# Copying and starting x's quarters one by one, and computing the last 128 tokens by tokens, in a conditioned residual block on one core

## The reference

```python
x = x + causal_depthwise_conv(x, cond[:, None, :])        # 32 taps, taps shared by all sequences
ada = (cond @ ada_w + ada_b)[:, None, :]
shift1, scale1, gate1, shift2, scale2, gate2 = split(ada, 6)
x1 = ln(x) * (1 + scale1) + shift1
q, k, v = split(x1 @ qkv_w + qkv_b)                       # 16 heads of 128
attn = softmax(q k^T / sqrt(128)) v                       # within a sequence of 32 tokens
x = x + gate1 * (attn @ out_w + out_b)
x2 = ln(x) * (1 + scale2) + shift2
h = gelu(x2 @ ffn_w1 + ffn_b1)                            # 1024 hidden channels
x = x + gate2 * (h @ ffn_w2 + ffn_b2)
```

## Time and profile before

| | us |
|---|---|
| median of 3 runs | 304.48 (304.09 to 304.70) |
| the profiled execution's own time | 304.34 |
| its span in the trace | 302.5 |
| PE busy | 295.8 |
| DVE busy | 183.0 |
| ACT busy | 171.4 |
| POOL busy | 121.8 |
| last product of TensorE starts | 298.06 |

### The profile page before, as it was taken

How to read it: one execution, slowest core, us unless ns; L and a number is a source line. 1 busy time by engine, 2 the same in 40 slices (tenths; PEclk the granted TensorE clock), 3 DMA queues, 4 the chain that set the end, 5 groups by cost and what they waited for, 6 DMA issues and landing times.

```text
span 302.5 us, 6172 instructions
## 1 busy us (share of the span) xinstructions
PE 295.8 (98%) x2598; PEld 250.0 (83%) x2598; DVE 183.0 (60%) x323; ACT 171.4 (57%) x310; POOL 121.8 (40%) x104
## 2 busy tenths in 40 slices
PE   7999999999999999999999999999999999999994
PEld 7896898878898888788888888888888888877884
DVE  3997697997867648472446664350721364859533
ACT  5953377534862765485267736644763695624910
POOL 5207839331811553172337134630916381321410
PEclk9999999999999999999999999999999999999998
DMA  7912422400250061007003400520090000000404
GB/s 227 367 41 71 119 91 70 142 0 2 62 217 0 4 210 71 0 2 277 3 2 111 168 0 2 177 103 0 4 339 8 2 0 3 0 1 2 69 0 69
DMA packets 22427, 23.00 MB, mean 76 GB/s; under 512 B 9240, under 2 KB 15488, under 8 KB 22400
## 3 DMA queue, kind: packets, MB, share of 16 engines
q1 hardware_dynamic: 20720, 22.39, 22.6%
q10 hardware_dynamic: 1680, 0.23, 0.4%
HBM read 21.57 MB, written 1.05 MB: 75 GB/s over the span
## 4 chain that ended last, share of the span: by engine, by line
PE 85%; DVE 11%; POOL 1%; issue 1%; ACT 0%; DVEq 0%; POOLq 0%
PE bank L1051 16%; PE bank L1052 16%; PE bank L1053 16%; PE bank L1139 8%; DVE xc L591 6%; PE bank L1059 5%; PE bank L1061 5%; PE bank L1060 5%; PE bank L1123 3%; PE bank L1267 3%; PE bank L1269 2%; PE bank L1268 2%; DVE pt L741 1%; DVE ol L746 1%; POOL wl L314 1%; PE bank L1010 1%
## 5 line engine op out<-in xcount | busy, mean ns | idle before, releaser
L314 POOL TENSOR_TENSOR wl<-raw,wh 128x512 fp32r<-128x512 f32 x70 | 96.0, 1396 | 119.2 <-ACT wh L387 100.8
L442 ACT ACTIVATE pool<-bank,bT 128x512 f32<-128x512 f32 x56 | 38.5, 688 | 50.4 <-PE bank L1053 50.4
L1051 PE MATMUL bank<-x1h,wl 128*128 128x512 f32 (+1 forms) x180 | 66.8, 371 | 0.0
L1052 PE MATMUL bank<-x1l,wh 128*128 128x512 f32 (+1 forms) x180 | 65.7, 365 | 0.0
L1053 PE MATMUL bank<-x1h,wh 128*128 128x512 f32 (+1 forms) x180 | 65.6, 365 | 0.0
L746 DVE SCALAR_TENSOR_TENSOR ol<-bank,bT,oh 128x512 fp32r<-128x512 f32 x32 | 23.9, 749 | 31.6 <-ACT oh L467 30.8
L591 DVE SCALAR_TENSOR_TENSOR xc<-x,condT,xc 128x496 f32<-128x496 f32 (+27 forms) x76 | 39.9, 593 | 0.1
L387 ACT ACTIVATE wh<-raw 128x512 fp32r<-128x512 f32 x70 | 39.8, 622 | 0.0
L1051 PEld LDWEIGHTS bank<-x1h,wl 128*128 128x128 f32 x180 | 34.0, 189 | 6.4 <-issue 1.0
L1053 PEld LDWEIGHTS bank<-x1h,wh 128*128 128x128 f32 x180 | 34.0, 189 | 5.5
L1052 PEld LDWEIGHTS bank<-x1l,wh 128*128 128x128 f32 x180 | 34.0, 189 | 5.0
(11 more groups left out here) (136 smaller groups left out, 426.0 us busy)
## 6 DMA issues: line engine op xcount, KB each, us to landing
raw<-in_L_cond_qkv_w_dram SPq DMA_DIRECT2D x24, 512.0 KB, 5.7
raw<-in_L_cond_out_w_dram SPq DMA_DIRECT2D x8, 512.0 KB, 3.6
raw<-in_L_cond_ffn_w_dram SPq DMA_DIRECT2D x3, 512.0 KB, 7.0
adaw<-in_L_cond_ada_w_dram SPq DMA_DIRECT2D x1, 1024.0 KB, 10.3
out_dram<-pool SPq DMA_DIRECT2D x12, 64.0 KB, 1.9
xtok<-in_x_dram SPq DMA_DIRECT2D x2, 256.0 KB, 3.1
adaw<-in_L_cond_ada_w_dram SPq DMA_DIRECT2D x1, 512.0 KB, 5.2
xtok<-in_x_dram SPq DMA_DIRECT2D x1, 512.0 KB, 6.0
```

Source lines behind the costliest of these rows:

```text
L314: g.tensor_tensor(wl[:, cols], raw[:, cols], wh[:, cols].bitcast(F32), ALU.subtract)\
L442: a.activation((q_sb if j < GH else k_sb)[:, j % GH, :], src, ACT.Identity, bias=bias(U, j // GH, j % GH)).then_inc(s_ev, 1)
L1051: pe.matmul(dst, wl[:, w_cols], a_hi, start=start, stop=False)
L1052: pe.matmul(dst, wh[:, w_cols], a_lo, start=False, stop=False)
```

## The change

Two changes are made at once. At the start, each of the four pieces of x (two quarters times two channel groups) gives its own signal when it is turned; the second quarter is turned into banks `PB[0]` and `PB[2]`. VectorE copies only the first piece, ScalarE the other three. VectorE then runs the first lag (lag 0) as four steps of 256 tokens, and TensorE its first lag (lag 13) as four products of 256 tokens, each behind its own piece. TensorE's three idle products go.

At the end, the last 128 tokens (the last four sequences) are taken out of pieces 2 and 3, which now cover 384 tokens each, and the old piece 4 goes. In its place `ffn2_last` multiplies the other way round: `hh` and `hl` of the 128 tokens are the stationary operand, the weights' 256 columns move, and the result has tokens as rows. What it has to be multiplied by and added to must then have tokens as rows too: `last_rest_by_blocks` on VectorE makes gate2 times bias plus residual for the 128 tokens, and transposes that and gate2 in blocks of 32 x 32, between hidden tiles 5 and 7; 16 transfers from SBUF to SBUF, all on SP, put the blocks in their places (`pexp`). The result is then one multiplication and one addition over 256 columns, and is stored by two transfers of 64 rows of 1 KB each, one on SP and one on ScalarE's queue. No transpose follows.

```diff
-        ALL, FRONT, BACK = slice(0, HT), slice(0, HT // 2), slice(HT // 2, HT)
-        FFN2_PIECES = [(0, 0, YB[0][:, ALL], ALL), (0, 1, YB[1][:, ALL], ALL), (1, 0, YB[0][:, ALL], ALL),
-                       (1, 1, YB[1][:, FRONT], FRONT), (1, 1, PB[0][:, FRONT], BACK)]
+        X_BANKS = [OB, (PB[0], PB[2])]
+        ALL, FRONT, BACK = slice(0, HT), slice(0, HT - P), slice(HT - P, HT)
+        FFN2_PIECES = [(0, 0, YB[0][:, ALL], ALL), (0, 1, YB[1][:, ALL], ALL), (1, 0, YB[0][:, FRONT], FRONT),
+                       (1, 1, YB[1][:, FRONT], FRONT)]
+        last_turned = pn[:, :].rearrange("p (q f) -> p q f", q=2 * CT)
+        last_rest, last_gate, last_rows = pe_[:, 0:C], pe_[:, C:2 * C], sd[:, 0:C]
...
 @block.sync
-            for n, ct in ((0, 0), (0, 1), (1, 0)):
-                sp.wait_ge(s_turn, CT * n + ct + 1)
+            for ct in range(CT):
+                sp.wait_ge(s_turn, ct + 1)
                 for i in range(P // T):
-                    store_blocks(sp, n, ct, i, ALL)
-            sp.wait_ge(s_turn, 5)
+                    store_blocks(sp, 0, ct, i, ALL)
+            sp.wait_ge(s_lturn, 2 * CT)
+            for b in range(QB):
+                for i in range(P // T):
+                    sp.dma_start(pe_[T * b:T * (b + 1), :].rearrange("t (q i c) -> t q i c", i=P // T, c=T)[:, :, i, :],
+                                 last_turned[T * i:T * (i + 1), :, T * b:T * (b + 1)]).then_inc(s_lrows, 16)
+            sp.wait_ge(s_turn, 3)
+            for i in range(P // T):
+                store_blocks(sp, 1, 0, i, FRONT)
+            sp.wait_ge(s_turn, 4)
             for i in range(2):
-                store_blocks(sp, 1, 1, i, BACK)
+                store_blocks(sp, 1, 1, i, FRONT)
+            sp.wait_ge(s_fin, 5)
+            store_last(sp, 0)
...
 @block.scalar
-            for n in range(2):
-                a.wait_ge(s_xt, n + 1)
-                a.activation(part(x0, 1, CHUNKS[n]), (OB, YB)[n][1][:, 0:256], ACT.Copy).then_inc(s_xe[1], 1)
+            for n, ct in ((0, 1), (1, 0), (1, 1)):
+                a.wait_ge(s_xt, CT * n + ct + 1)
+                a.activation(part(x0, ct, CHUNKS[n]), X_BANKS[n][ct][:, 0:256], ACT.Copy).then_inc(s_xe[1], 1)
...
 @block.vector
+            v.tensor_copy(part(x0, 0, CHUNKS[0]), X_BANKS[0][0][:, 0:256]).then_inc(s_xe[0], 1)
             for n in range(2):
-                v.wait_ge(s_xt, n + 1)
-                v.tensor_copy(part(x0, 0, CHUNKS[n]), (OB, YB)[n][0][:, 0:256]).then_inc(s_xe[0], 1)
-                if n == 0:
-                    first_lag(0)
+                for ct in range(CT):
+                    if (n, ct) == (0, 0):
+                        v.wait_ge(s_xe[0], 1)
+                    else:
+                        v.wait_ge(s_xe[1], CT * n + ct)
+                    xs = part(x0, ct, CHUNKS[n])
+                    v.scalar_tensor_tensor(out=part(xc, ct, CHUNKS[n]), in0=xs, scalar=condT[:, ct, T - 1:T], in1=xs,
+                                           op0=ALU.mult, op1=ALU.add).then_inc((s_cfirst, s_cdve)[n], 1)
...
+            def last_rest_by_blocks():
+                for ct in range(CT):
+                    v.scalar_tensor_tensor(out=rest, in0=ada(GATE2, ct, LAST_SPAN),
+                                           scalar=bT[:, B_F2 + ct:B_F2 + ct + 1],
+                                           in1=by_batch(part(xc, ct, LAST_SPAN)), op0=ALU.mult, op1=ALU.add)\
+                        .then_inc(s_lbias, 1)
+                    v.wait_ge(s_lbias, ct + 1)
+                    v.transpose(by_batch(last_turned[:, ct, :]), rest).then_inc(s_lturn, 1)
+                    v.transpose(by_batch(last_turned[:, CT + ct, :]), ada(GATE2, ct, LAST_SPAN)).then_inc(s_lturn, 1)
...
-            gated(4)
-            turn(4)
+            v.wait_ge(s_f2, 5)
+            v.wait_ge(s_lrows, 16 * QB * P // T)
+            v.tensor_tensor(last_rows, LAST_BANK, last_gate, ALU.mult).then_inc(s_gt, 1)
+            v.wait_ge(s_gt, 5)
+            v.tensor_tensor(last_rows, last_rows, last_rest, ALU.add).then_inc(s_fin, 1)
...
 @block.tensor
-                m.then_inc(s_xt, 1)
+                    m.then_inc(s_xt, 1)
-            idle_products(3)
...
+            def first_lag():
+                j = PE_LAGS[0][0]
+                for n in range(2):
+                    for ct in range(CT):
...
+                        t0 = CHUNKS[n][0]
+                        pe.matmul(by_batch(CONV_BANK[0][ct][:, t0:t0 + 256])[:, :, j:], diag[:, ct, :],
+                                  by_batch(part(x0, ct, CHUNKS[n]))[:, :, :T - j], start=(n == 0), stop=False)
...
-            conv(0, 0, 6)
+            first_lag()
+            conv(0, 1, 6)
...
+            def ffn2_last(k):
+                pe.matmul(LAST_BANK, hh[:, k, BACK], w_lo, start=(k == 0), stop=False)
+                pe.matmul(LAST_BANK, hl[:, k, BACK], w_hi, start=False, stop=False)
+                m = pe.matmul(LAST_BANK, hh[:, k, BACK], w_hi, start=False, stop=(k == MT - 1))
```

More of the change, by code:

```diff
@@ L227, in store_blocks, with store_last @@
                 .then_inc(s_out, 16)
+        def store_last(eng, i):
+            rows_i = slice(i * P // 2, (i + 1) * P // 2)
+            eng.dma_start(out[B_LAST:B].rearrange("b t c -> (b t) c")[rows_i], last_rows[rows_i]).then_inc(s_out, 16)
         block = ctx.enter_context(nc.Block())
@@ L550, in _ @@
             a.wait_ge(s_turn, 4)
-            for i in range(P // T):
+            for i in range(2, P // T):
                 store_blocks(a, 1, 1, i, FRONT)
-            a.wait_ge(s_turn, 5)
-            for i in range(2, P // T):
-                store_blocks(a, 1, 1, i, BACK)
+            a.wait_ge(s_fin, 5)
+            store_last(a, 1)
         @block.vector
@@ L561, in _ @@
                 .then_inc(s_cond, 1)
[L562 to L574 removed]
+            v.wait_ge(s_xt, 1)
+            v.tensor_copy(part(x0, 0, CHUNKS[0]), X_BANKS[0][0][:, 0:256]).then_inc(s_xe[0], 1)
+            v.wait_ge(s_cond, 1)
+            for n in range(2):
+                for ct in range(CT):
[6 more added lines that the diff above has]
+                                           op0=ALU.mult, op1=ALU.add).then_inc((s_cfirst, s_cdve)[n], 1)
             def conv(n, i0, i1):
@@ L579, in conv @@
                     for ct in range(CT):
-                        if n == 0 and i == 0 and ct == 0:
-                            first_lag(1)
-                            continue
                         xs = by_batch(half(x0, ct, n))
@@ L585, in conv @@
                         w = condT[:, ct, T - 1 - j:T - j]
-                        if n == 0 and i == 1 and ct == 0:
-                            v.wait_ge(s_cfirst, 1)
+                        if n == 0 and i == 1:
+                            v.wait_ge(s_cfirst, ct + 1)
                         if i:
@@ L928, in turn @@
                             by_batch(half(x0, ct, n)[:, toks])).then_inc(s_turn, 1)
+            def last_rest_by_blocks():
+                v.wait_ge(s_pt, QB * (NU + 1))
+                for ct in range(CT):
+                    rest = by_batch(part(x0, ct, LAST_SPAN))
+                    v.wait_ge(s_lo, CT * (NC + 1) + ct + 1)
+                    v.wait_ge(s_xs, CT + ct + 1)
+                    v.scalar_tensor_tensor(out=rest, in0=ada(GATE2, ct, LAST_SPAN),
[5 more added lines that the diff above has]
+                    v.transpose(by_batch(last_turned[:, CT + ct, :]), ada(GATE2, ct, LAST_SPAN)).then_inc(s_lturn, 1)
             gated(0)
@@ L936, in _ @@
             hidden_low(1, 5)
+            last_rest_by_blocks()
             hidden_low(1, 7)
@@ L962, in _ @@
                     for t in range(nt):
-                        m = pe.transpose((OB, YB)[n][ct][:, t * P:(t + 1) * P], xtok[:, t0 + t, ct * P:(ct + 1) * P], ident[:, :])
-                m.then_inc(s_xt, 1)
-            idle_products(3)
+                        m = pe.transpose(X_BANKS[n][ct][:, t * P:(t + 1) * P], xtok[:, t0 + t, ct * P:(ct + 1) * P],
+                                         ident[:, :])
+                    m.then_inc(s_xt, 1)
             def conv(n, i0, i1):
@@ L1298, in _ @@
             pe.wait_ge(s_gt, CT)
-            for piece in (2, 3, 4):
+            for piece in (2, 3):
                 for k in range(MT):
                     ffn2(piece, k)
+            for k in range(MT):
+                ffn2_last(k)
 _INS = ['x', 'cond_2048', 'L1_cond_ada_w', 'L1_cond_ada_b', 'L1_cond_qkv_w', 'L1_cond_qkv_b', 'L1_cond_out_w',
```

38 lines of the change are left out of this document (25 added, 13 removed).

## The result

The kernel after takes **307.03 us** (median of five runs, 307.01 to 307.56), the kernel before 304.09 in the runs beside it. The ratio is 1.0095, 95% interval 1.0084 to 1.0107: slower by 2.9 us, where 303.5 was forecast. The profiled execution took 307.01, with a span of 305.2 against 302.5.

A forecast was written before the change was run, and what follows sets the result against it. TensorE, with 85% of the span, was taken as the bound, leaving only the chain's departures from it and the tail. Start -0.7 and tail -0.2 made -0.9 on a span of 302.5: 303.5 us forecast, range 302.4 to 304.6.

The forecast's parts named there:

- SP's queue: Tail: 16 new transfers issued 0.49 us apart (0.44 to 0.55), then six stores; tail -0.2 us, bounds -1.1 to +1.1.
- The last store: End of SP's queue: issued near 299.5, about 0.9 us behind VectorE's last step, landing 1.6 to 1.9 later.
- The third rival: Tail: the 16 transfers on SP become the bound from a pitch of 0.585 us; 306.0 at 0.65; chance 0.12.
- The start: From x's copies to VectorE's sum with TensorE's part: -0.7 us, from -0.4 to -0.85, carried to the end.
- the 0.68 us that the prediction gives TensorE: Start: TensorE gains 0.68 us, its 19 lags ending at 20.1 instead of 20.78.
- The idle products: Start, TensorE: its first lag starts at 5.79 instead of at 6.91 behind three idle products.
- The last products: TensorE's products at the end: 11.27 us in all as before, no change; the last one near 297.4.
- The blocking of VectorE by GpSimd's step: Tail: VectorE's second new multiplication, about 1.2 us long beside GpSimd's step, puts the transposes' end at 289.3, unblocked 288.4.
- The two transposes of 128 columns: Tail, among VectorE's six new steps: an estimated 0.31 us for each transpose.
- Hidden tile 7: Tail: VectorE makes it from 289.3 to 290.0, 0.6 us before piece 2 asks for it: no cost.

The follow-up runs named there:

- e15: Kernel after with SP's first four stores of a finished piece cut into 16 of 128 runs; 310.44 us.
- e16: Kernel after with SP's 14 stores of finished pieces built with `nc.dge_precook = False`; 307.65 us.
- e17: Kernel after with the 16 transfers replaced by 16 of 64 runs to the output in DRAM, in a pattern of two batches of 32 partitions; 303.57 us.
- e3: Kernel after with the 16 transfers shared between SP and ScalarE's queue; 303.39 us, ratio 0.9975 to the kernel before.
- e8: Kernel after with the 16 transfers unbroken on both sides and split over SP and ScalarE's queue; 303.35 us, ratio 0.9970 to the kernel before.
- e14: Kernel after with eight transfers of 256 runs in place of the 16; 303.62 us.
- e18: e8 with the last two stores cut by columns in place of rows; 303.33 us, ratio 0.9961 to the kernel before.
- e11: Kernel after with SP's six stores behind the 16 transfers issued by ScalarE's queue; 305.83 us.
- e1: Kernel before with the change at the start alone; 303.70 us, ratio 0.9989.
- e12: Kernel after with GpSimd's diagonals started only when VectorE has done its small lags; 310.4 us.
- e10: Kernel after with the 16 transfers cut to 64 runs each and read from x in DRAM, still written to SBUF; 307.26 us.
- e4: Kernel after with VectorE's six new steps one step sooner, ahead of hidden tile 5; 304.09 us, ratio 0.9997 to the kernel before.
- e9: Kernel after with the 16 transfers cut to 64 runs each and written from SBUF to the output in DRAM; 306.83 us.
- e7: Kernel after with both sides of the 16 transfers unbroken, 512 bytes in each of 32 partitions; 306.32 us.
- e6: Kernel after with the 16 transfers carrying only the rest's blocks and not the gate's, half the runs; 306.74 us.

## Why the prediction was wrong

**SP's queue: the step that failed.** The prediction said: "The 16 new transfers have 128 runs each, which by that line is 0.49; nothing in the trace is a transfer from SBUF to SBUF, so the bounds are 0.44 and 0.55." The line of stores from 512 over 256 down to 128 runs was right for stores (0.475 in e15). What I took for a law of size held for stores as this kernel builds them: e16's, of the same sizes, were 0.65 to 0.67 apart. The pitch of the transfers was 0.643. By this step's own working the first transfer was due at 288.6 (289.3 less the 0.7 of the start), the last at 295.95; they came at 288.43 and 298.26. The last one is 2.3 us late: 2.3 from 15 pitches of 0.643, 0.2 more because the first pitch was 0.83, and 0.2 less because the first transfer started 0.17 early. The bounds were too narrow as well: an operation that the trace did not show at all, 16 times over, deserved wider bounds than the spread of the stores. The rows that I used were of stores from SBUF to DRAM alone, 0.50 to 0.56 apart; none of them has the pitch of 0.643.

**The last store: sized too small.** Forecast for 299.5, it was issued at 302.49. Of these 3.0 us the transfers make 2.6: 2.3 as above, and 0.3 because the last transfer holds the queue for 0.64 and the sum had counted 0.37 for it. The rest is a gap of 0.43 between the sixth store and the last (302.06 to 302.49) that I had not seen coming. By e15 the gap belongs neither to this store nor to its wait. In all twelve runs in which SP issues 78 transfers in the program it stands before the 78th, with 0.40 to 0.43 us (0.40 in e17 behind stores 0.51 to 0.54 apart, 0.42 in e16 behind stores 0.65 to 0.67 apart). In e15, with 90 issues, the 78th is the 11th of the 16 transfers, and the 0.43 us stand there; before its last store SP rests 0.04 (306.19 to 306.23), although that store too waits for a signal that had long come. Runs with 70 or 72 issues (e3, e8, e14, e18, e11) have no 78th. So the gap goes with the place in the queue's program; what it is, and what the long 12th transfer of e15 is, stays open. Then the last store landed 2.32 later, not 1.6 to 1.9: the two stores of 64 rows of 1 KB land 2.0 to 2.3 us behind their issue, those that I had as rows 1.6 to 1.9. 3.0 + 0.5 = 3.5 us, from 303.5 to 307.0.

**The third rival was what happened.** It was worked out as one from a pitch of 0.585 on, "at 0.65 the kernel takes 303.4 + 2.6 = 306.0". The mechanism and its place, SP's queue, were right; the gap and the landing, 0.43 + 0.5, make the rest to 307.0. VectorE's wait at L979 alone, which the rival named beside it, would have ended 1.7 us sooner. Its chance of 0.12 was too low: I set it against stores with four times the runs, the same comparison that failed.

**The start: right in kind, too large.** Forecast -0.7 from -0.85 to -0.4; e1 measured -0.37, just outside (its interval is -0.6 to -0.1). The small lags are 0.51 apart and not 0.44, as e12 shows by taking GpSimd away. The working had this effect for steps of 496, with its size, and left it out for the small ones: over the four of them that cost 0.3 us. VectorE's sum was 0.41 earlier and not 0.75. No run shows the 0.68 us that the prediction gives TensorE here: its first lag was through at 7.33, where the next product starts, and at 7.94 in the kernel before, so it gained 0.61. The row's 5.80 + 1.70 = 7.50 is the end of the lag's last pass, which starts at 7.20 and lasts 0.29.

**Right.** The idle products were no loss: the passes of TensorE's first lag stand 0.25 us apart up to 6.81 and 0.13 from there on, and the idle products of the kernel before went from 0.21 to 0.15 apart at 6.65, nearly as early. The moment is not the same in every execution; in e1's the transposes of x went from 0.21 to 0.11 apart at about 5.5. The last products: TensorE's last one was forecast at 297.4 and stood at 297.30, 11.15 us behind the first one of piece 2, as in the kernel before (11.17). That their absolute times fit is in part luck: piece 2 began at 286.15, 0.74 earlier than before, but VectorE's sum was 0.41 earlier and e1 gained 0.37. The rest is scatter of the middle: in the runs with the new start the last product lies between 297.25 (e8) and 298.07 (e10), if e12 is left out. The blocking of VectorE by GpSimd's step: the second new multiplication took 1.43 beside GpSimd's step from 286.43 to 287.72 and ended at 287.87; 289.3 for the end of the transposes was 288.6 after the start's gain, measured 288.41. It hung on little: VectorE's step started 0.01 behind GpSimd's (286.44 and 286.43), where the working had 0.2. The same step without a neighbour, at 285.63, took 0.34 us and not 1.43. The two transposes of 128 columns took 0.31 and 0.27, where 0.31 was estimated. Hidden tile 7 cost nothing, as said: VectorE made its low part from 288.33 to 288.98.

## What to carry to other kernels

Price the issue of a DMA by its kind before you price its size: with 128 runs each, the stores of e15 were 0.475 us apart and the transfers 0.643. When the new issues are of a kind that your rows don't have, the rows are no bound, above all with 16 of them in a row: measure one such issue first. A queue that stands before the last store is part of the end: count its issues from the first one behind the last wait, and compare with when the result is ready. Such a queue is cheaply relieved by the other one (e3: 3.6 us), or by starting it one step sooner (e4: 2.9 us).

## What the hardware showed that I had not expected

- The cost of an issue depended little on what was moved. The transfers to the rows' tile and those of e9 were 0.633 (32 runs, 16 KB, e7) to 0.652 us apart (256 runs, 32 KB, e14), and e16's stores of 512 runs (64 KB) 0.66 to 0.67. The stores of e17 were 0.470 apart (64 runs), those of e15 0.475 (128 runs), those of the kernel after 0.51 (384 runs) and 0.53 to 0.56 (512 runs). SBUF on both sides made no difference of its own: 0.639 in e6, 0.638 in e9 and 0.637 in e10 for the same 64 runs.
- Two queues that issued transfers at the same time kept their pitch (0.65 each in e3). What a store beside them costs differs: ScalarE's second store lasted 0.71 in the kernel after, 0.57 in e9 and 0.49 in e7, with SP's transfers beside it, and 0.49 in e3, where SP issued stores at that time; in e11, beside SP's transfers, the stores behind the first of a group lasted 0.50 to 0.74.
- One line of the build, `nc.dge_precook = False` in e16, took the same stores from 0.49 to 0.63 us an issue. The last store lasted 0.55 us cut by rows (the kernel after) and 0.36 cut by columns (e18).
- A queue can stand still at a fixed place in its program: SP did for 0.40 to 0.43 us before its 78th issue, in twelve runs before the last store and in e15 in the middle of the 16 transfers.
- GpSimd's diagonals and VectorE's steps slow each other: in the kernel after, diagonals of 0.38 us become 0.53 beside small lags and 0.78 beside steps of 496; small lags take 0.48 without them (e12) and 0.59 with them.
